# Routing the head mixture in two halves of eight token tiles, inside the neighbouring blocks

## The chip, the cores and the metric

The kernel runs on one core of one Trainium2 chip. The metric is the device time of one execution in microseconds (us). The core has five engines with queues of their own: PE (matrix products, its weight loads shown apart as PEld), DVE (vector work), ACT (activations, copies, scaling), POOL (elementwise work, here mostly powers and splits) and SP (issues DMAs). They meet only at semaphores and at barriers.

## The reference

Two layers over a batch of 4 sequences of 2048 tokens with 256 features. Layer 0 is a wave mixer with a residual and a layer norm, and then the head mixture that the change touches; layer 1 (a state-space scan and a small mixture of experts) stays as it is. What the head mixture computes for x, the output of the first layer norm:

```
logits = normalize(x) @ normalize(sim) - sigmoid(gates)      # 16 experts per token
gated  = relu(logits);  mask = gated > 0
if no expert of a token is active: mask = the 2 largest logits
rw     = softmax(where(mask, gated, -inf))                   # routing weights
q,k,v  = sum over experts of rw[e] * (x @ W_e)               # 3 x 64 columns per expert
attn   = causal softmax(q k^T / 8) v
y      = sum over experts of rw[e] * (attn @ O_e)
x      = layer_norm(x + y)
```

## The kernel before

Layer 0 runs once for each of the 4 sequences, in a loop on the device. Tokens lie in 16 tiles of 128. The names in the code: `tok` holds the tokens (16 tiles of 128x256), `xT` their transpose, `simn` the normalized expert directions, `wmoh` the expert weights as a rounded part and a remainder, `rw` the routing weights.

An iteration is a row of blocks. A block gives each engine an order of its own, and no engine goes to the next block before all have ended the present one (a barrier). The blocks that matter, in order:

- **The wave branch's second block.** PE makes the output projection tile by tile into six PSUM banks, `bank(i % 6)`; DVE adds each to `tok` and, group by group of four tiles, takes statistics (`ln1.statistics`) and scales (`ln1.scale`, L106); POOL makes the roots between them (`ln1.root`, L100); PE transposes the scaled group (L119) and ACT copies the transposes to `xT` (`ln1.copy`, L126), two tiles at a time.
- **The gating block** (L544 to L611). ACT squares and sums all 16 tiles (L558), POOL takes one root of all 16 sums (L566), PE makes the logits of all tiles (L549, against `simn` padded to 128 columns), and DVE turns them into `rw` in one chain of operations on all tiles (L574 to L611), with one exponential by ACT (L561).
- **The tile loop.** For each of 16 tiles, ACT rounds a tile of `xT` (`round_x`, L713), POOL makes its remainder (L639), PE makes six slabs of 512 columns, six matmuls each (L663), and the weighted sum over the experts is taken by ACT for experts 0 to 3 (`weigh`, L721) and by DVE for 4 to 15 (L689), followed by L695 to L702 and, two tiles later, L676 and L678. PE works one tile ahead: a slab of tile i waits until the slab of tile i-1 in its bank has been read (semaphores `pa` and `pu`). `flip` transposes q and k of the tile before into banks 6 and 7.
- The attention and output blocks, which the change leaves alone.

The order on each engine is written out by hand; no scheduler moves anything.

Of the kernel before, what the change touches and what calls it, by code (L numbers as in the profile page):

```python
# [10 lines left out]
ALU = mybir.AluOpType  # L11
# [140 lines left out]
def layer0(nc, t, out, top, tile, sem, sems, clear, bank, ident, ones, half_pow, layer_norm, kpad, x2_dram,  # L152
           x2T_dram):
    with ExitStack() as L:
# [190 lines left out]
        tok = tile(L, "tok", [P, TILES, D])  # L345
        with nc.Fori(0, BATCH) as b:
            with ExitStack() as s:
                wave_branch(nc, t, b, s, tile, sem, bank, ident, tok, xT, wqkvg, bq, bg_half, bout, wout, toep,
                            cct, layer_norm)
            with ExitStack() as s:  # L350
                head_mixture(nc, t, b, s, tile, sem, bank, ident, half_pow, tok, xT, wmoh, wo, simn, gate_sig, causal,
                             ident_bf,
                             layer_norm, x2_dram, x2T_dram)
            clear(outside)


def wave_branch(nc, t, b, s, tile, sem, bank, ident, tok, xT, wqkvg, bq, bg_half, bout, wout, toep, cct,
                layer_norm):
# [3 lines left out]
    dep_late = tile(s, "dep_late", [P, 2, CHUNK])  # L362
    tmp = tile(s, "feat_tmp", [P, 2, 5, CHUNK])
    qf = tile(s, "qf", [P, 2, CHUNK])
# [3 lines left out]
    lastg = tile(s, "lastg", [P, KC])  # L368
    proj, feat, used = sem("proj_ready"), sem("feat_ready"), sem("proj_used")
# [75 lines left out]
    wd, mm, su = sem("wave_done"), sem("wout_ready"), sem("wout_used")  # L445
    ln1 = layer_norm("ln1", s, tok, xT)
    with nc.Block() as block:
        @block.tensor
        def _(pe):

# [21 lines left out]
            for i in range(TILES):  # L472
                pe.wait_ge(wd, i // 4 + 1)
                if i >= 6:
                    pe.wait_ge(su, i - 5)
                for k in range(KC):
                    last = pe.matmul(bank(i % 6)[:, 0:D],
                                     qg[:, k, i * P:(i + 1) * P], wout[:, k, :], start=(k == 0), stop=(k == KC - 1))
# [7 lines left out]
        def _(act):  # L486
# [3 lines left out]
            for g in range(TILES // 4):  # L490
                ln1.copy(act, g)

        @block.gpsimd
        def _(pool):
            for g in range(TILES // 4):
                ln1.root(pool, g)

        @block.vector
        def _(dve):
# [16 lines left out]
            for g in range(TILES // 4):  # L516
                for i in range(4 * g, 4 * g + 4):
                    dve.wait_ge(mm, i + 1)
                    dve.tensor_tensor(tok[:, i, :], tok[:, i, :], bank(i % 6)[:, 0:D], ALU.add).then_inc(su, 1)
# [6 lines left out]
def head_mixture(nc, t, b, s, tile, sem, bank, ident, half_pow, tok, xT, wmoh, wo, simn, gate_sig, causal, ident_bf,  # L526
                 layer_norm, x2_dram, x2T_dram):
# [9 lines left out]
    with ExitStack() as g:  # L537
# [3 lines left out]
        ss, rs = tile(g, "ss", [P, TILES]), tile(g, "rs", [P, TILES])  # L541
        sq = tile(g, "sq", [P, 2, D])
        sr, sp_, lr, le, lx = (sem(n) for n in ("norm_sums", "norm_root", "logits_mm", "logits", "logits_exp"))
        with nc.Block() as block:  # L544
            @block.tensor
            def _(pe):
                for i in range(TILES):
                    for k in range(KC):
                        last = pe.matmul(bank(0, 4)[:, i * P:(i + 1) * P], xT[:, k, i * P:(i + 1) * P],  # L549
                                         simn[:, k, :], start=(k == 0), stop=(k == KC - 1))  # L550
                last.then_inc(lr, 1)

            @block.scalar
            def _(act):
                for i in range(TILES):
                    if i >= 2:
                        act.wait_ge(sr, i - 1)
                    act.activation(sq[:, i % 2, :], tok[:, i, :], ACT.Square, accum_out=ss[:, i:i + 1])\  # L558
                       .then_inc(sr, 1)
                act.wait_ge(le, 1)  # L560
                act.activation(ex[:, :, :], lg[:, :, :], ACT.Exp).then_inc(lx, 1)  # L561

            @block.gpsimd
            def _(pool):
                pool.wait_ge(sr, TILES)
                pool.tensor_tensor(rs[:, :], ss[:, :], half_pow[:, :], ALU.pow).then_inc(sp_, 1)  # L566

            @block.vector
            def _(dve):
                def wide(a):  # L570
                    return a.unsqueeze(2).broadcast_to([P, TILES, EXPERTS])

                dve.wait_ge(sp_, 1)
                dve.tensor_scalar(rs[:, :], rs[:, :], 1e-12, None, ALU.max)  # L574
                dve.drain()
                dve.reciprocal(rs[:, :], rs[:, :])
                dve.drain()
                dve.wait_ge(lr, 1)
                dve.tensor_tensor(lg[:, :, :], bank(0, 4).rearrange("p (i e) -> p i e", e=P)[:, :, 0:EXPERTS],
                                  wide(rs[:, :]), ALU.mult)  # L580
                dve.drain()
                dve.tensor_tensor(lg[:, :, :], lg[:, :, :],
                                  gate_sig[:, :].unsqueeze(1).broadcast_to([P, TILES, EXPERTS]), ALU.subtract)\
                   .then_inc(le, 1)
                dve.drain()

                for i in range(TILES):
                    dve.max(top8[:, i, :], lg[:, i, :])
                dve.drain()
                dve.tensor_copy(best[:, :], top8[:, :, 0])  # L590
                dve.drain()
                dve.memset(top8[:, :, 2:8], -3e38)
                dve.drain()
                for i in range(TILES):
# [1142 lines left out]
```

## Time and profile before

| | |
|---|---|
| median of 3 runs | 4489.09 us (4488.7 to 4492.88) |
| the profiled execution | 4494.44 us |
| its span, first to last instruction | 4492.6 us |
| mean granted TensorE clock | 0.925 of full |
| PE, DVE, POOL, ACT busy | 80%, 72%, 40%, 31% of the span |

The shares are averages over stages with very different limits: a long scan in layer 1, and the short stages of layer 0 around the change. The change must be read from its own stage, in which most engines stand still. Times below are from the span's start; the second of the four iterations stands for all, and what differs in the others is shown.

### The profile page before, as it was taken

How to read it: one execution, taken by the hardware profiler on the slowest of the kernel's cores; microseconds unless marked ns; L12 is line 12 of the kernel's file. 1: busy time of each engine (PE TensorE's matmuls, PEld its weight loads, DVE VectorE, ACT ScalarE, POOL GpSimd, SP SyncE). 2: the span in 40 equal slices, each digit the busy share in tenths (PEclk: the TensorE clock that was granted, in tenths of full speed). 3: DMA queues.
4: the chain of work that ended last, by engine and by line, in shares of the span. 5: the costliest groups of instructions: out<-in, count | busy, mean ns of one | idle time of the engine just before them, and what ended most of it. 6: DMA issues, size and time to landing. Idle time of an engine off the chain costs nothing. (4 is left out here: it accounts for less than half of the span.)

```text
span 4492.6 us, 39616 instructions
## 1 busy us (share of the span) xinstructions
PE 3576.0 (80%) x13112; PEld 2012.1 (45%) x13168; DVE 3243.8 (72%) x4803; ACT 1407.8 (31%) x2360; POOL 1796.4 (40%) x874
## 2 busy tenths in 40 slices
PE   5799879987988798777778677777777786777769
PEld 2577557765766486632223322224322233222234
DVE  4566456545754476469997679995699976799955
ACT  3222322232223222253332343331533323433310
POOL 1101210121003000309995049991099950499910
PEclk9899989998989899899999889998999998899989
DMA  3000100010001000206663136661066631366530
GB/s 126 1 19 1 57 1 10 10 57 1 1 20 58 1 1 19 90 11 217 209 206 131 34 123 211 210 202 61 10 218 209 207 131 35 122 209 209 204 107 7
DMA packets 156471, 421.74 MB, mean 94 GB/s; under 512 B 21713, under 2 KB 58961, under 8 KB 154465
## 3 DMA queue, kind: packets, MB, share of 16 engines
q1 hardware_dynamic: 156258, 419.03, 27.4%
q8 instruction: 118, 1.93, 0.2%
q14 instruction: 95, 0.78, 0.1%
HBM read 392.20 MB, written 26.78 MB: 93 GB/s over the span
## 5 line engine op out<-in xcount | busy, mean ns | idle before, releaser
L1376 POOL TENSOR_TENSOR hc<-h,c_sb 128x1024 f32<-128x1024 f32 x344 | 806.0, 2352 | 622.5 <-DMA c_sb<-bc_rows 550.7
L1304 PE MATMUL PS<-hc,ident 128*128 128x512 f32 x1376 | 712.4, 644 | 89.7 <-POOL hc L1376 75.0
L1345 ACT ACTIVATE da<-dt,a_neg 128x1024 f32<-128x1024 f32 x384 | 437.7, 1141 | 501.5 <-DVE h L1401 501.4
L1287 PE MATMUL PS<-bc,pick 128*128 128x512 bf16 x712 | 237.5, 414 | 300.6 <-DVE h L1401 265.8
L1384 DVE TENSOR_TENSOR PS<-dtu,PS 128x1024 f32<-128x1024 f32 x384 | 461.4, 1202 | 5.4 <-PE PS L1287 5.4
L1304 PEld LDWEIGHTS PS<-hc,ident 128*128 128x128 f32 x1376 | 257.7, 200 | 425.2 <-issue 207.8
L1401 DVE TENSOR_TENSOR_SCAN h<-da,state,PS 128x1024 f32<-128x1024 f32 x192 | 443.3, 2328 | 0.0
L1401 DVE TENSOR_TENSOR_SCAN h<-da,PS 128x1024 f32<-128x1024 f32 x192 | 431.3, 2268 | 0.0
L100 POOL TENSOR_TENSOR ln_rstd<-ln_var,eps_pow 128x4 f32<-128x4 f32 x65 | 71.4, 1105 | 849.8 <-DVE ln_var L93 849.8
L689 DVE SCALAR_TENSOR_TENSOR acc<-PS,rw,acc 128x192 f32<-128x192 f32 x768 | 285.0, 413 | 174.5 <-ACT acc L721 91.1
L1376 POOL TENSOR_TENSOR tok<-h,c_sb 128x1024 f32<-128x1024 f32 x168 | 395.1, 2352 | 33.7 <-DVE h L1401 24.5
L1304 PE MATMUL PS<-tok,ident 128*128 128x512 f32 x672 | 345.2, 638 | 44.7 <-POOL tok L1376 39.0
L885 POOL TENSOR_TENSOR mix<-attn,rw 128x1024 f32<-128x1024 f32 x64 | 121.3, 1904 | 517.5 <-POOLq L753 464.4
L1287 PEld LDWEIGHTS PS<-bc,pick 128*128 128x128 bf16 x768 | 57.9, 103 | 588.4 <-DVE h L1401 501.5
L663 PE MATMUL PS<-wmoh_hi,xhi 128*128 128x512 f32 x768 | 250.6, 408 | 49.1 <-POOL xlo L639 49.1
L392 PE MATMUL PS<-xT,wqkvg 128*128 128x512 f32 x512 | 234.9, 622 | 57.1 <-issue 28.2
L663 PE MATMUL PS<-wmoh_lo,xhi 128*128 128x512 f32 x768 | 243.5, 398 | 0.0
L663 PE MATMUL PS<-wmoh_hi,xlo 128*128 128x512 f32 x768 | 243.0, 398 | 0.0
L1091 PE MATMUL PS<-u,w_dt 128*128 128x512 f32 x512 | 230.9, 609 | 12.4 <-DVE dt L1217 12.4
L639 POOL TENSOR_TENSOR xlo<-xT,xhi 128x256 fp32r<-128x256 f32 x64 | 46.8, 735 | 450.3 <-ACT xhi L713 450.3
L1304 PEld LDWEIGHTS PS<-tok,ident 128*128 128x128 f32 x672 | 126.3, 200 | 203.6 <-POOL tok L1376 97.9
L1352 ACT ACTIVATE state<-h 128x1 f32<-128x1 f32 x256 | 51.9, 203 | 474.3 <-DVE h L1401 474.3
(251 smaller groups left out, 6552.1 us busy)
## 6 DMA issues: line engine op xcount, KB each, us to landing
c_sb<-bc_rows SPq DMA_DIRECT2D x512, 512.0 KB, 4.2
bu<-bc_rows SPq DMA_DIRECT2D x64, 512.0 KB, 5.4
tok<-bc_rows SPq DMA_DIRECT2D x64, 512.0 KB, 5.5
xT<-in_xT SPq DMA_DIRECT2D x5, 2048.0 KB, 7.5
tok<-in_x SPq DMA_DIRECT2D x4, 2048.0 KB, 9.6
x_after_layer<-tok SPq DMA_DIRECT2D x16, 512.0 KB, 3.0
xT_after_layer<-x2T_out SPq DMA_DIRECT2D x16, 512.0 KB, 2.8
x2T<-xT_after_layer SPq DMA_DIRECT2D x16, 512.0 KB, 3.7
```

What stands on the lines that cost most here:

```text
L100: pool.tensor_tensor(rstd[:, w], var[:, w], eps_pow[:, w], ALU.pow).then_inc(rstd_ready, 1)
L392: last = pe.matmul(bank(4 * (u % 2) + kind), wqkvg[:, k, m * P:(m + 1) * P], xT[:, k, n * CHUNK:(n + 1) * CHUNK], start=(k == 0), stop=(k ...
L663: last = pe.matmul(bank(j), x[:, i % 2, k, :], wmoh[part][:, k, j * CHUNK:(j + 1) * CHUNK], start=(q == 0), stop=(q == len(passes) - 1))
L689: op = dve.scalar_tensor_tensor(acc[:, i % 2, e % 4, :], expert(e), rw[:, i, e:e + 1], acc[:, i % 2, e % 4, :], ALU.mult, ALU.add)
L885: pool.tensor_tensor(mix[:, i % 2, :, :], attn[:, i, :].unsqueeze(1).broadcast_to([P, EXPERTS, EHD]), rw[:, i, :].unsqueeze(2).broadcast_t ...
L1091: last = pe.matmul(bank(where + j)[0:rows, :], weights(k), u[:, k, n * CHUNK:(n + 1) * CHUNK], start=(k == 0), stop=(k == KI - 1))
L1287: op = pe.matmul(bank(at + j), pick[:, row, :], bc3[:, half * HALF + j * CHUNK:half * HALF + (j + 1) * CHUNK], start=True, stop=True)
L1304: op = pe.matmul(bank(Y + j), ident[:, :], hc_at[v % 3][:, j * CHUNK:(j + 1) * CHUNK], start=(n == 0), stop=(n == N - 1))
L1345: act.activation(decay_at(v), dt[:, m, at], ACT.Exp, scale=a_neg[:, n:n + 1]).then_inc(dr, 1)
L1376: pool.tensor_tensor(hc_at[v % 3], h[:, v % 3, :], c_sb[:, v % 3, :], ALU.mult).then_inc(hr, 1)
L1384: dve.tensor_tensor(b_bank(v), dtu[:, m, at], b_bank(v), ALU.mult).then_inc(bd, 1)
L1401: dve.tensor_tensor_scan(h[:, v % 3, :], decay_at(v), bu_at[on_pool.index(v) % 2] if v in on_pool else b_bank(v), first, ALU.mult, ALU.add ...
```

## The change

It does five things. The squares and sums of the norms are taken by ACT in the wave branch's second block, four tiles behind each scaled group, and the roots by POOL in four operations of four columns, in that block too. The logits of tiles 0 to 7 are made there by PE as well, with 16 columns in place of 128, into bank 5, so the output projection has five banks. The gating block is gone. The chain that makes `rw` is called twice, each time for eight tiles: at the head of DVE's tile loop, and between its tiles 0 and 1. The logits of tiles 8 to 15 are made by PE behind the slabs of tile 0, into bank 7.

```diff
+            def logits(g):
+                pe.wait_ge(ln1.copied, 2 * g + 2)
+                for i in range(4 * g, 4 * g + 4):
+                    for k in range(KC):
+                        last = pe.matmul(bank(5)[:, i * EXPERTS:(i + 1) * EXPERTS], xT[:, k, i * P:(i + 1) * P],
+                                         simn[:, k, 0:EXPERTS], start=(k == 0), stop=(k == KC - 1))
+                last.then_inc(lr, 1)
...
-                if i >= 6:
-                    pe.wait_ge(su, i - 5)
+                if i >= 5:
+                    pe.wait_ge(su, i - 4)
...
+            logits(0)
+            logits(1)
             ln1.transpose(pe, 2)
             ln1.transpose(pe, 3)
...
             for g in range(TILES // 4):
+                act.wait_ge(ln1.done, g + 1)
+                for i in range(4 * g, 4 * g + 4):
+                    if i >= 2:
+                        act.wait_ge(sr, i - 1)
+                    act.activation(sq[:, i % 2, :], tok[:, i, :], ACT.Square, accum_out=ss[:, i:i + 1])\
+                       .then_inc(sr, 1)
                 ln1.copy(act, g)
...
+            def norm(g):
+                w = slice(4 * g, 4 * g + 4)
+                pool.wait_ge(sr, 4 * g + 4)
+                pool.tensor_tensor(rs[:, w], ss[:, w], half_pow[:, w], ALU.pow).then_inc(sp_, 1)
+
             for g in range(TILES // 4):
                 ln1.root(pool, g)
+                if g >= 2:
+                    norm(g - 2)
+            norm(TILES // 4 - 2)
+            norm(TILES // 4 - 1)
...
                     for j in range(SLABS):
+                        if i == 0 and j == 5:
+                            pe.wait_ge(lt, 1)
...
+                    if i == 0:
+                        logits(2)
+                        logits(3)
+                    if i == 2:
+                        pe.wait_ge(lt, 2)
...
+                gating(0)
                 for i in range(TILES):
+                    if i == 1:
+                        gating(1)
...
                 def weigh(i):
+                    if i % (TILES // 2) == 0:
+                        act.wait_ge(gd, 1 + i // (TILES // 2))
...
                 round_x(0)
                 round_x(1)
+                exp_logits(0)
                 for i in range(TILES):
                     weigh(i)
                     if i + 2 < TILES:
                         round_x(i + 2)
+                    if i == 0:
+                        exp_logits(1)
```

`gating(half)` holds the statements of the old DVE chain, with every slice narrowed to eight tiles; it signals `lt` once the logits have been read from PSUM and `gd` once `rw` stands. `exp_logits(half)` is the old exponential, of eight tiles.

ACT's queue from the wave branch's second block to the second tile of the tile loop, in the kernel before:

```order
L126 ACTIVATE xT<-PS 128x2x256 x8
L447 UNCONDITIONAL_BRANCH
L553 UNCONDITIONAL_BRANCH
L558 ACTIVATE sq,ss<-tok 128x256 x16
L561 ACTIVATE ex<-lg 128x256
L544 UNCONDITIONAL_BRANCH
L708 UNCONDITIONAL_BRANCH
L713 ACTIVATE xhi<-xT 128x256 x2
L721 ACTIVATE acc<-PS,rw 128x192 x4
```

The same stretch of ACT's queue in the changed kernel (L510 is the square, L126 the copy to `xT`, L735 the rounding, L756 the exponential, L745 `weigh`):

```order
L510 ACTIVATE sq,ss<-tok 128x256 x4
L126 ACTIVATE xT<-PS 128x2x256 x2
L510 ACTIVATE sq,ss<-tok 128x256 x4
L126 ACTIVATE xT<-PS 128x2x256 x2
L452 UNCONDITIONAL_BRANCH
L730 UNCONDITIONAL_BRANCH
L735 ACTIVATE xhi<-xT 128x256 x2
L756 ACTIVATE ex<-lg 128x128
L745 ACTIVATE acc<-PS,rw 128x192 x4
L735 ACTIVATE xhi<-xT 128x256
L756 ACTIVATE ex<-lg 128x128
```

The squares now stand between the copies, four ahead of each pair, and the second exponential ahead of the second tile's weighing.

DVE's queue behind tile 0 of the tile loop, in the kernel before (L699 and L702 end tile 0, L689 is tile 1's weighted sum):

```order
L699 TENSOR_TENSOR v<-acc 128x64
L702 TENSOR_TENSOR qk<-acc 128x256
L689 SCALAR_TENSOR_TENSOR acc<-PS,rw,acc 128x192 [waits weighed_by_act,slab_ready]
L689 SCALAR_TENSOR_TENSOR acc<-PS,rw,acc 128x192 [waits slab_ready]
L689 SCALAR_TENSOR_TENSOR acc<-PS,rw,acc 128x192 x2
```

The same place in the changed kernel (L721 and L724 end tile 0, L661 onward is the gating chain of tiles 8 to 15):

```order
L721 TENSOR_TENSOR v<-acc 128x64
L724 TENSOR_TENSOR qk<-acc 128x256
L661 TENSOR_SCALAR rs<-rs 128x8 [waits norm_root]
L663 RECIPROCAL rs<-rs 128x8
L666 TENSOR_TENSOR lg<-PS,rs 128x128 [waits logits_mm]
L669 TENSOR_TENSOR lg<-lg,gate_sig 128x128
L675 MAX top<-lg 128x8 x8
L677 COPY best<-top 128x8
```

Tile 1's weighted sum now stands behind the whole second gating chain, which itself waits for PE's logits.

PE's queue at the end of tile 0's slabs, in the kernel before:

```order
L663 MATMUL PS<-wmoh_hi,xhi 128x512 x2
L663 MATMUL PS<-wmoh_lo,xhi 128x512 x2
L663 MATMUL PS<-wmoh_hi,xlo 128x512 x2
L663 MATMUL PS<-wmoh_hi,xhi 128x512 [waits weighed_by_act,x_lo_ready]
L663 MATMUL PS<-wmoh_hi,xhi 128x512
```

And in the changed kernel (L631 is a matmul of the slabs, L616 one of the logits):

```order
L631 MATMUL PS<-wmoh_hi,xhi 128x512 [waits logits_taken]
L631 MATMUL PS<-wmoh_hi,xhi 128x512
L631 MATMUL PS<-wmoh_lo,xhi 128x512 x2
L631 MATMUL PS<-wmoh_hi,xlo 128x512 x2
L616 MATMUL PS<-simn,xT 128x16 x16
L631 MATMUL PS<-wmoh_hi,xhi 128x512 [waits weighed_by_act,x_lo_ready]
L631 MATMUL PS<-wmoh_hi,xhi 128x512
```

The last slab of tile 0 waits until DVE has read the first half's logits, and sixteen matmuls of 16 columns stand ahead of tile 1. (Each f32 matmul of these lists is two MATMUL records in the trace.)

## Rows read from the trace of the kernel before

**Rows 1.** Timeline of PE, first and second iteration (start us, us, engine, line, operation, [idle before])
```profile
181.75 1.22 PE L663 MATMUL PS<-wmoh_hi,xhi 128*128 128x512 f32 x2 [11.47 <-POOL xlo L639]
...
588.06 9.76 PE L477 MATMUL PS<-wout,qg 128*128 128x256 f32 x44 [1.26 <-DVE qg L514]
...
611.44 3.48 PE L119 MATMUL PS<-ident,tok 128*128 128x128 f32 x16 [3.99 <-DVE tok L106]
615.85 7.38 PE L549 MATMUL PS<-simn,xT 128*128 128x128 f32 x64 [0.94 <-PEq L447]
636.37 1.22 PE L663 MATMUL PS<-wmoh_hi,xhi 128*128 128x512 f32 x2 [13.13 <-POOL xlo L639]
```

**Rows 2.** Timeline of ACT, first and second iteration
```profile
191.98 0.42 ACT L713 ACTIVATE xhi<-xT 128x256 fp32r<-128x256 f32 x1 [4.84 <-PE PS L663]
...
606.18 1.08 ACT L126 ACTIVATE xT<-PS 128x512 f32<-128x512 f32 x2 [4.88 <-PE PS L119]
...
614.95 0.60 ACT L126 ACTIVATE xT<-PS 128x512 f32<-128x512 f32 x1 [0.26 <-PE PS L119]
615.83 0.42 ACT L558 ACTIVATE sq<-tok 128x256 f32<-128x256 f32 x1 [0.28 <-PEq L447]
...
634.70 0.72 ACT L713 ACTIVATE xhi<-xT 128x256 fp32r<-128x256 f32 x2 [7.41 <-PEq L544]
...
647.86 0.42 ACT L713 ACTIVATE xhi<-xT 128x256 fp32r<-128x256 f32 x1 [5.23 <-PE PS L663]
...
664.84 0.42 ACT L713 ACTIVATE xhi<-xT 128x256 fp32r<-128x256 f32 x1 [4.86 <-PE PS L663]
```

**Rows 3.** Timeline of POOL, second iteration
```profile
622.41 2.90 POOL L566 TENSOR_TENSOR rs<-ss,half_pow 128x16 f32<-128x16 f32 x1 [10.99 <-ACT sq L558]
...
635.59 1.41 POOL L639 TENSOR_TENSOR xlo<-xT,xhi 128x256 fp32r<-128x256 f32 x2
```

**Rows 4.** Timeline of DVE, second iteration
```profile
610.01 2.83 DVE L106 TENSOR_SCALAR tok<-tok,ln_mv,ln_rstd 128x256 f32<-128x256 f32 x8
625.34 0.17 DVE L574 TENSOR_SCALAR rs<-rs 128x16 f32<-128x16 f32 x1 [12.50 <-POOL rs L566]
...
626.93 1.32 DVE L588 MAX8 top<-lg 128x8 f32<-128x16 f32 x16
...
628.84 0.09 DVE L595 MATCH_VALUE_LOAD rep<-top,lg 128x8 f32 x1
...
631.31 0.29 DVE L597 TENSOR_SCALAR fb<-rep 128x256 f32<-128x256 f32 x1
...
633.92 0.43 DVE L611 TENSOR_TENSOR rw<-ex,ss 128x256 f32<-128x256 f32 x1
642.80 0.42 DVE L689 SCALAR_TENSOR_TENSOR acc<-PS,rw,acc 128x192 f32<-128x192 f32 x1 [8.46 <-ACT acc L721]
...
649.81 0.42 DVE L702 TENSOR_TENSOR qk<-acc 128x256 f32<-128x256 f32 x1
```

**Rows 5.** Single lines over the run (ns min/median/max, first and last start us)
```profile
L100 POOL TENSOR_TENSOR ln_rstd<-ln_var,eps_pow x65: 1006/1017/1247, 140.0 to 4487.0; 128x4 f32<-128x4 f32 x65
L676 DVE TENSOR_TENSOR q_parts<-PS,q_parts x64: 294/295/295, 211.4 to 1696.6; 64x128 fp32r<-64x128 f32 x64
```

**Rows 6.** PE timeline of the wave branch's convolution, second iteration
```profile
572.86 9.52 PE L462 MATMUL PS<-toep,dpad 128*32 128x512 f32 x128 [0.58 <-DVE dpad L505]
```

**Rows 7.** Windows, second iteration (us, busy time per engine and count, PEclk, DMA share, GB/s)
```profile
607.45:611.40 3.95, 0.00 (x0) 0.00 (x0) 3.65 (x14) 0.00 (x0) 1.22 (x1) 1.00 0.00 0
611.40:615.80 4.40, 3.48 (x16) 2.70 (x16) 1.38 (x4) 2.39 (x4) 0.02 (x1) 0.61 0.00 0
636.30:642.50 6.20, 6.13 (x14) 4.78 (x15) 0.00 (x0) 1.34 (x4) 0.70 (x2) 0.50 0.01 3
656.20:782.00 125.80, 121.41 (x537) 97.92 (x535) 89.46 (x248) 31.58 (x101) 9.57 (x13) 0.99 0.00 1
```

**Rows 8.** The page's groups: busy us, mean ns | idle of the engine before them, releaser
```profile
L663 PE MATMUL PS<-wmoh_hi,xhi 128*128 128x512 f32 x768 | 250.6, 408 | 49.1 <-POOL xlo L639 49.1
```

More of the change, by code:

```diff
@@ L368, in wave_branch @@
     lastg = tile(s, "lastg", [P, KC])
+    first = s.enter_context(ExitStack())
+    dep_late = tile(first, "dep_late", [P, 2, CHUNK])
+    tmp = tile(first, "feat_tmp", [P, 2, 5, CHUNK])
+    qf = tile(first, "qf", [P, 2, CHUNK])
     proj, feat, used = sem("proj_ready"), sem("feat_ready"), sem("proj_used")
@@ L445, in wave_branch @@
     wd, mm, su = sem("wave_done"), sem("wout_ready"), sem("wout_used")
+    sr, sp_, lr = (sem(n) for n in ("norm_sums", "norm_root", "logits_mm"))
+    first.close()
+    sq = tile(s, "sq", [P, 2, D])
     ln1 = layer_norm("ln1", s, tok, xT)
@@ L518, in _ @@
                     dve.wait_ge(mm, i + 1)
-                    dve.tensor_tensor(tok[:, i, :], tok[:, i, :], bank(i % 6)[:, 0:D], ALU.add).then_inc(su, 1)
+                    dve.tensor_tensor(tok[:, i, :], tok[:, i, :], bank(i % 5)[:, 0:D], ALU.add).then_inc(su, 1)
                 ln1.statistics(dve, g)
@@ L540, in head_mixture @@
         best = tile(g, "best", [P, TILES])
[L541 to L594, printed above, removed]
-                    dve.match_replace(rep[:, i, :], top8[:, i, :], lg[:, i, :], 1e30)
-                dve.drain()
-                dve.tensor_scalar(fb[:, :, :], rep[:, :, :], 1e29, None, ALU.is_gt)
-                dve.tensor_scalar(best[:, :], best[:, :], 0.0, None, ALU.is_le)
-                dve.drain()
-                dve.tensor_tensor(fb[:, :, :], fb[:, :, :], wide(best[:, :]), ALU.mult)
-                dve.wait_ge(lx, 1)
-                dve.scalar_tensor_tensor(ex[:, :, :], lg[:, :, :], 0.0, ex[:, :, :], ALU.is_gt, ALU.mult)
-                dve.drain()
-                dve.tensor_tensor(ex[:, :, :], ex[:, :, :], fb[:, :, :], ALU.add)
-                dve.drain()
-                dve.tensor_reduce(ss[:, :], ex[:, :, :], AX.X, ALU.add)
-                dve.drain()
-                dve.reciprocal(ss[:, :], ss[:, :])
-                dve.drain()
-                dve.tensor_tensor(rw[:, :, :], ex[:, :, :], wide(ss[:, :]), ALU.mult)
@@ L614, in head_mixture @@
-    with ExitStack() as g:
+        sp_, lr, lt, le, lx = (sem(n) for n in ("norm_root", "logits_mm", "logits_taken", "logits", "logits_exp"))
+        gd = sem("weights_done")
         acc = tile(g, "acc", [P, 2, 4, QKV])
@@ L651, in flip, with logits @@
                     last.then_inc(qt, 1)
+                def logits(g):
+                    for i in range(4 * g, 4 * g + 4):
+                        at = (i - TILES // 2) * EXPERTS
+                        for k in range(KC):
+                            last = pe.matmul(bank(7)[:, at:at + EXPERTS], xT[:, k, i * P:(i + 1) * P],
+                                             simn[:, k, 0:EXPERTS], start=(k == 0), stop=(k == KC - 1))
+                    last.then_inc(lr, 1)
                 passes = [(x, part, k) for x, part in ((xhi, 0), (xhi, 1), (xlo, 0)) for k in range(KC)]
```

59 lines of the change are left out of this document (51 added, 8 removed).

## The prediction

> **What bounds the kernel now.** I read the page first, for the span, then the timelines of the four engines between the wave branch and the tile loop of the second iteration, then windows for the granted clock. The page says only that no engine is full; what counts is which wait ends last in this stage. Around the change the kernel is a serial chain that hands the work from engine to engine. ACT ends its last copy at 614.95 + 0.60 = 615.55 and, behind the barrier, starts the squares at 615.83 [rows 2]; POOL starts the root of all sixteen at 622.41 [rows 3]; DVE starts the gating at 625.34 and ends it at 633.92 + 0.43 = 634.35 [rows 4]; ACT rounds at 634.70 [rows 2], POOL makes two remainders from 635.59 [rows 3], and PE starts the slabs at 636.37, 13.13 us after its own logits ended [rows 1]. PE is the only heavy engine of what follows and is the one kept waiting: over the four iterations it idles 49.1 us ahead of the first slab [rows 8], with its 7.38 us of logits [rows 1] beside the squares on top. From the first slab on, the tile loop is paced by PE: 121.41 busy of 125.80 us, while DVE has 89.46 [rows 7].
>
> I call T0 the start of the tile loop's block (ACT's first rounding), 634.70 now. PE starts at T0 + 1.67.
>
> **The change, part by part.**
>
> *The squares move behind the scaled groups.* Sixteen take 622.41 - 615.83 = 6.58 us, so a group of four takes 1.65 [rows 2, 3]. The first two groups cost nothing: ACT idles 4.88 us ahead of its copies there [rows 2]. The last two lie on the path. DVE scales groups 2 and 3 in one run of 2.83 us from 610.01, so group 2 is done near 611.4 and group 3 at 612.84 [rows 4]. ACT: squares 611.4 to 613.05, two copies (1.08 for two [rows 2]) to 614.15, squares to 615.8, copies to 616.9. It ends 1.35 us later than the 615.55 of now. PE's transposes are ready before ACT asks for them.
>
> *The roots.* A root of four columns takes 1.02, at most 1.25 us [rows 5]. Three of the four have cover: the one for group 0 stands ahead of the last layer-norm root, but its sums are there some 9 us earlier, and POOL is idle. The last starts at 615.85 and ends between 616.9 and 617.1, beside ACT's last copies. With the barrier (0.35 from DVE's end to ACT's start now, [rows 2, 4]) T0 becomes 617.1 + 0.3 = 617.4. **That is 634.70 - 617.4 = 17.3 us earlier.** The 2.90 us root of 16 columns, the squares, DVE's 9.01 us of gating and one barrier are all out of the path ahead of T0.
>
> *Logits of the first half, on PE.* They fill the gap in which PE now stands idle, 3.99 us ahead of 611.44 [rows 1]; only the second four wait for ACT's copies, which the squares delay from 607.26 [rows 2] to about 608.9. In the trace they are 32 records. Even at the 0.115 us each of the 128-column ones (7.38 / 64 [rows 1]) tiles 4 to 7 end by 610.8. If they end later, up to 1.7 us of it is covered by ACT's squares of group 2. Cost 0.
>
> *Five banks in place of six.* PE makes a tile of the projection in 4 x 9.76 / 44 = 0.89 us [rows 1] and now waits for the add five tiles back. Tile 5 would start at 592.5, tile 9 at 596.0; in between DVE has only one statistics group, of some 2 us, and behind tile 10 PE waits for the scaled group anyway. Cost 0; what hides it is that wait.
>
> *Gating of the first half, now inside the tile loop.* DVE's chain takes 634.35 - 625.34 = 9.01 us. Halved, the maxima save 0.66 of 1.32, the replacements half of 631.31 - 628.84 = 2.47, so 1.2 [rows 4], and seven operations of 256 elements at 0.43 [rows 4] go to the 0.295 that one of 128 elements takes [rows 5], 0.9 together. That leaves 6.2 us. Behind it on DVE's queue is tile 0's weighted sum, and ACT's four scalings wait for it too, at most 1.7 us (0.42 each, as its 256-element rounding takes [rows 2]). So DVE can start its sum at T0 + 7.9. Now it starts at 642.80, T0 + 8.1 [rows 4], since the slabs come no earlier: the gating hides behind PE's first slabs. PE's tile 0 needs only that the logits have been read before slab 5, at about T0 + 1.1. Cost 0. Uncovered it would be 6.2.
>
> *Logits of the second half.* This is the part that I put on the path: 32 records on PE between tile 0 and tile 1, where PE is the pace. The trace has no run of 16-column f32 matmuls in a stream. The nearest from above are the 128-column ones, 0.115 each, 3.7 us. Matmul time follows the columns (256 take 0.222, 128 take 0.115 [rows 1]), which would make 16 columns 0.014 each, 0.5 us, but every record has a weight load of 128x128 of its own, so something holds above that. The convolution's mixed records on 32-column weights come every 9.52 / 128 = 0.074 us [rows 6]. I take 0.074: **2.4 us per iteration**, bounds 0.5 and 3.7. The Trainium skill, TensorE: Matmul & The Clock Gate, section Back-to-back issue gap, puts streams of weight load and matmul at about 81 ns each for 128 columns; by that price, called an estimate, the part would be 2.6 us. No row here shows such a stream at 16 columns.
>
> *Gating of the second half.* It starts on DVE behind tile 0, at T0 + 15.5 (649.81 + 0.42 = 650.23 now [rows 4]), just when the logits are ready (T0 + 13.2 + 2.4), and ends at T0 + 21.8. Tile 1's sum would otherwise have started at about T0 + 19, so DVE is 2.8 us late. Does PE stop? PE runs tile 1 from T0 + 15.6 to 24, and needs DVE's reads only for slab 1 of tile 2, at about T0 + 25.5; DVE has read slab 1 of tile 1 by T0 + 22.7. It has 2.5 us of every 8.6 to catch up with ((125.80 - 89.46) over 14.6 tiles [rows 7]), and is level within tile 2. ACT's second exponential waits for DVE too, with the second tile's scalings behind it, done by T0 + 19. Cost 0, cover some 2.8 us.
>
> A sentence that the sum can do without: the Trainium skill, SBUF — State Buffer, section SBUF: two separate sides, says that a DVE operation with two SBUF inputs and a GpSimd one that reads SBUF exclude each other. Gating's subtraction now falls beside POOL's first remainder, which PE's start waits for. By that rule the sum would be up to 0.3 us per iteration smaller; no row here shows those two side by side.
>
> *The clock.* The slabs start at the low level: from 636.30 to 642.50 the granted clock is 0.50 (1.2 GHz), later 0.99 [rows 7]. From the first slab to ACT's rounding at the end of tile 0 it is 647.86 - 636.37 = 11.49 us, in the first iteration 191.98 - 181.75 = 10.23, at full speed (664.84 - 647.86) / 2 = 8.49 [rows 1, 2]. PE's idle time ahead of the slabs shrinks from 13 to about 4 us (last transpose near 615.2, slab at 619.1). An idle time of 3.95 us is in the trace, and 0.61 on average is granted right after it [rows 7]. So I let tile 0 keep its time.
>
> **The sum.** 17.3 - 2.4 = 14.9 us per iteration, 59.6 in four. The profiled execution, 4494.4 us (span 4492.6), would become 4434.8; it lies 5.3 us above the median of the runs. From that median, 4489.1 - 59.6 = **4429.5 us**.
>
> **The rivals.**
> 1. *The clock stays up* through the short idle time. Tile 0 then saves 1.7 to 3.0 us per iteration, 9 in all: 4420. For it: idle falls from 13 to 4 us and PE was busy before. Against: the row of 3.95 us.
> 2. *The second gating stops PE*: DVE's 2.8 us lateness goes through, and the logits cost 3.7. 4 x (2.8 + 1.3) = 16 us back: 4446. For it: PE runs only one tile ahead. Against: the margin of some 2.8 us worked out above.
> 3. *The loop falls into another step and gives all back.* If DVE, started late, never catches up and PE waits at every tile for a bank, each of the 15 later tiles must grow by 14.9 / 15 = 0.99 us (8.6 to 9.6) to cancel the gain; 0.15 us more per tile makes it 4498, slower. Against: DVE's 2.5 us of slack per tile, and no instruction of the later tiles has changed.
> 4. *The work only changes place*: the gating turns out to be what the first tile waits for, 6.2 us exposed. 4 x 6.2 = 25 back: 4454. Against: it ends at T0 + 6.2, while the slabs pace DVE to T0 + 13 either way.
>
> **How the numbers follow.** Main case 0.52, rival 1 0.20, rival 2 0.16, rival 4 0.05, rival 3 0.04 (half of it slower), small unknowns 0.03. The range runs from rival 1 with cheaper logits, 4414, to rival 2, 4447. The three runs span 4 us, so 0.2%, 9 us, is about what can be told from no change. Faster 0.94, same 0.03, slower 0.03.
>
> **What would show it.** Right: the squares stand between the copies and the wave block's last copy ends near 617; the gating block is gone and PE's idle time ahead of the first slab falls from 49.1 to near 16 us in all; 32 logit records take about 2.4 us behind tile 0; PE has no wait on DVE in tile 2. Wrong: a clock of 1.00 in the first slabs (faster), PE waiting on DVE's reads in tiles 1 to 3 (slower), or ACT's copies ending well behind 617.

## The result, and the profile after

| | before | after |
|---|---|---|
| median of the runs, us | 4488.9 (4484.25 to 4492.88, 4 runs) | 4443.15 (4441.28 to 4445.53, 4 runs) |
| ratio of after to before | | 0.9899, 95% interval 0.9882 to 0.9916 |
| profiled execution, its span | 4494.44, 4492.6 | 4445.53, 4443.7 |
| mean granted clock | 0.925 | 0.925 |

The change made the kernel 45.7 us faster by the medians, 48.9 by the profiled executions (the one of the kernel before lies 5.5 us above its median, the changed one 2.4). Forecast was 59.6.

PE in the second iteration, timeline (start us, us, engine, line, operation, count, [idle before]):

```profile
579.03 9.76 PE L490 MATMUL PS<-wout,qg 128*128 128x256 f32 x44 [1.26 <-DVE qg L544]
...
598.24 4.55 PE L460 MATMUL PS<-simn,xT 128*128 128x16 f32 x32
602.63 4.02 PE L119 MATMUL PS<-ident,tok 128*128 128x128 f32 x16
609.89 1.22 PE L631 MATMUL PS<-wmoh_hi,xhi 128*128 128x512 f32 x2 [3.24 <-POOL xlo L597]
...
619.96 0.62 PE L631 MATMUL PS<-wmoh_hi,xlo 128*128 128x512 f32 x2
620.42 3.64 PE L616 MATMUL PS<-simn,xT 128*128 128x16 f32 x32
623.91 0.70 PE L631 MATMUL PS<-wmoh_hi,xhi 128*128 128x512 f32 x2
624.45 0.87 PE L631 MATMUL PS<-wmoh_lo,xhi 128*128 128x512 f32 x2
625.12 1.05 PE L631 MATMUL PS<-wmoh_hi,xlo 128*128 128x512 f32 x2
```

ACT in the same stretch, its last copies, the rounding at T0 and the scalings:

```profile
606.71 1.06 ACT L126 ACTIVATE xT<-PS 128x512 f32<-128x512 f32 x2
608.21 0.72 ACT L735 ACTIVATE xhi<-xT 128x256 fp32r<-128x256 f32 x2 [0.44 <-PEq L452]
...
615.61 1.35 ACT L745 ACTIVATE acc<-PS,rw 128x192 f32<-128x192 f32 x4 [4.60 <-DVE rw L698]
620.62 0.42 ACT L735 ACTIVATE xhi<-xT 128x256 fp32r<-128x256 f32 x1 [3.65 <-PE PS L631]
```

The two stages are set against each other by the output projection, whose first matmul the change leaves alone. From it to T0 it was 634.70 - 588.06 = 46.64 us [rows 1, 2]; now it is 608.21 - 579.03 = 29.18. T0 comes 17.5 us earlier, and 17.6 to 18.0 in the other three iterations. PE's idle time ahead of the first slab fell from 13.13 to 3.24 us here, and over the run, in the page's row of the slabs, from 49.1 [rows 8] to:

```profile
L631 PE MATMUL PS<-wmoh_hi,xhi 128*128 128x512 f32 x768 | 252.3, 410 | 12.7 <-POOL xlo L597 12.7
```

Not all of it is kept. ACT rounds a tile of `xT` whenever PE has ended a tile, so its roundings measure the tiles. Tile 0 ends 620.62 - 609.89 = 10.73 us behind the first slab (11.49 before [rows 1, 2]; means over four iterations 10.54 and 10.85). Tile 1 takes 13.5 us in every iteration, 8.37 before, and later tiles 8.62, 8.59 before. The windows from the last transposes to tile 1 (us, busy time per engine and count for PE, PEld, DVE, ACT, POOL, then granted clock, DMA share, GB/s):

```profile
602.60:606.60 4.00, 3.87 (x17) 3.15 (x17) 1.20 (x4) 3.95 (x17) 1.62 (x2) 0.50 0.00 0
606.70:609.85 3.15, 0.00 (x0) 0.00 (x0) 1.43 (x3) 1.79 (x6) 2.67 (x4) 0.50 0.00 0
609.90:614.80 4.90, 4.90 (x12) 3.92 (x13) 4.25 (x33) 0.31 (x1) 0.62 (x1) 0.54 0.00 0
614.90:620.40 5.50, 5.50 (x25) 4.45 (x24) 3.61 (x12) 1.35 (x4) 0.00 (x0) 1.00 0.00 0
620.50:624.00 3.50, 3.50 (x34) 3.50 (x33) 2.49 (x9) 0.42 (x1) 0.73 (x1) 1.00 0.02 5
624.00:628.20 4.20, 4.20 (x13) 3.29 (x13) 3.50 (x32) 1.04 (x3) 0.00 (x0) 0.59 0.00 2
628.40:634.00 5.60, 5.60 (x26) 4.47 (x25) 4.34 (x13) 0.73 (x2) 0.00 (x0) 1.00 0.00 0
```

The first row is the last sixteen transposes, which stand right behind the first half's logits: the granted clock is 0.50 there already, and they take 4.02 us. It fell while those logits ran and PE was never idle: 1.00 from 598.24 to 600.00, 0.65 on average from there to 602.60. The transposes have cover, so this fall costs nothing at T0. The fifth row is the second half's logits: PE is never idle, and the granted clock is 1.00. The sixth is the beginning of tile 1: PE is still never idle, but the granted clock is 0.59, and pairs of slab matmuls take up to 1.05 us in place of 0.63. So tile 1 pays twice: 623.91 - 620.42 = 3.49 us for the logits, and 5.16 - 3.49 = 1.7 us for a slow start that no term of the forecast held.

The account of the profiled executions: T0 gives 17.56 + 17.46 + 17.81 + 17.97 = 70.8 us. The loops, from first slab to last rounding, take 127.47 in place of 122.28 us on average, 20.8 in four. The remaining 1.1 us back lie in stages that the change leaves alone: the parts of the iterations between the tile loop and the next output projection are 4.7 us longer in all, what follows the last tile loop is 2.7 shorter, and what precedes the first output projection 0.9 shorter. That is 70.8 - 20.8 - 1.1 = 48.9. Such a part takes 284.4 to 288.7 us in all these kernels and differs by up to 3.5 us between iterations of one kernel; what moves it is open. A difference of a few microseconds between two totals is therefore read from the traced stage, from the output projection to the last rounding, before it is put down to an edit: 170.70 us on average before, 158.20 in the changed kernel.

DVE around T0 and behind tile 0, and POOL at T0:

```profile
608.23 0.93 DVE L661 TENSOR_SCALAR rs<-rs 128x8 f32<-128x8 f32 x1 [4.44 <-PEq L452]
...
609.90 0.77 DVE L669 TENSOR_TENSOR lg<-lg,gate_sig 128x128 f32<-128x128 f32 x1
...
615.28 0.29 DVE L698 TENSOR_TENSOR rw<-ex,ss 128x128 f32<-128x128 f32 x1
617.15 4.54 DVE L711 SCALAR_TENSOR_TENSOR acc<-PS,rw,acc 128x192 f32<-128x192 f32 x12 [1.57 <-ACT acc L745]
...
622.91 0.16 DVE L661 TENSOR_SCALAR rs<-rs 128x8 f32<-128x8 f32 x1
...
624.10 0.29 DVE L666 TENSOR_TENSOR lg<-PS,rs 128x128 f32<-128x128 f32 x1 [0.75 <-PE PS L616]
624.48 0.29 DVE L669 TENSOR_TENSOR lg<-lg,gate_sig 128x128 f32<-128x128 f32 x1
```

```profile
608.19 0.95 POOL L592 MEMSET v<- 128x1024 f32 x1 [0.31 <-POOLq L452]
609.10 1.42 POOL L597 TENSOR_TENSOR xlo<-xT,xhi 128x256 fp32r<-128x256 f32 x2
```

The same two DVE operations take 0.93 and 0.77 us beside POOL's fill and first remainder, and 0.16 and 0.29 behind tile 0. Two things follow: the first chain lasts 7.3 us, not 6.2, and the fill of `v` stands ahead of the remainder that PE waits for.

### The profile page after: what moved, and what is told of

The parts are those of the page before. It is cut to its first block and busy times, and to the rows that moved or that the text cites. A ratio compares the mean times of both kernels' runs of the same rounds, so it can differ in the third digit from the quotient of the medians.

```text
span 4443.7 us, 39720 instructions
## 1 busy us (share of the span) xinstructions
PE 3583.3 (81%) x13112; PEld 2014.6 (45%) x13168; DVE 3257.2 (73%) x4859; ACT 1406.3 (32%) x2364; POOL 1799.9 (41%) x886
## 5 line engine op out<-in xcount | busy, mean ns | idle before, releaser
L631 PE MATMUL PS<-wmoh_hi,xhi 128*128 128x512 f32 x768 | 252.3, 410 | 12.7 <-POOL xlo L597 12.7
L631 PE MATMUL PS<-wmoh_lo,xhi 128*128 128x512 f32 x768 | 246.6, 403 | 0.0
L631 PE MATMUL PS<-wmoh_hi,xlo 128*128 128x512 f32 x768 | 245.4, 401 | 0.0
```

Of the source, the lines that this page charges most:

```text
L631: last = pe.matmul(bank(j), x[:, i % 2, k, :], wmoh[part][:, k, j * CHUNK:(j + 1) * CHUNK], start=(q == 0), stop=(q == len(passes) - 1))
```

## The experiments

Each ran beside the kernel before. Times are medians with the ratio's 95% interval; tile lengths are the spacing of ACT's roundings, as above.

**1. Is tile 1's slow start due to the narrow matmuls?** Three edits on the changed kernel.

```diff
 e1_wide_logits: second half's logits 128 columns wide, into banks 6 and 7
-  last = pe.matmul(bank(7)[:, at:at + EXPERTS], xT[...], simn[:, k, 0:EXPERTS], ...)
+  last = pe.matmul(bank(6, 2)[:, at:at + P], xT[...], simn[:, k, :], ...)
-                    if i == 2:
+                    if i == 1:
                         pe.wait_ge(lt, 2)
 e2_no_second_logits
                     if i == 0:
-                        logits(2)
-                        logits(3)
 e10_64_columns: both halves, in the same banks 5 and 7
-  bank(7)[:, at:at + EXPERTS] ... simn[:, k, 0:EXPERTS]
+  bank(7)[:, at:at + 64]      ... simn[:, k, 0:64]
```

> The changed kernel, but the logits of tiles 8 to 15 are made with all 128 columns of simn, into banks 6 and 7. Theory A (the slow start of tile 1 comes from the stretch of narrow matmuls, in which PE streams few columns): the 32 records still take about 0.115 us each, 3.7 us, the granted clock is 1.00 in tile 1, tile 1 with the logits takes about 12.1 us in place of 13.5, and the kernel takes about 4437 us. Theory B (it is a late effect of the idle time ahead of the slabs): tile 1 is slow as before, with the logits 13.7 us, and the kernel takes 4444 us.

> The changed kernel without PE's logits of tiles 8 to 15; DVE's second gating runs on the first half's logits instead, so the routing weights of tiles 8 to 15 are not those of the reference. Theory A: both the 3.5 us of the records and the slow start go, tile 1 takes 8.4 us, 5.1 less per iteration, and the kernel takes about 4423 us. Theory B: only the 3.5 us go, tile 1 takes 10.1 us, 4429 us. Theory C (the second gating on DVE is what holds tile 1): tile 1 stays above 12 us.

> The changed kernel with 64 columns per tile in place of 16 in all the logits, in the same banks. The records take 0.11 us each either way. If 64 columns are wide enough, tile 1 with its logits takes 12.0 us as with 128 columns, and the kernel 4433 us; if the clock also stays up from the first half's logits until the slabs, tile 0 falls from 10.5 towards 8.6 us, 4426 us. If 64 columns still count as narrow: tile 1 stays at 13.5 us, 4443 us.

| | us | ratio | tile 0 (mean) | tile 1 | later |
|---|---|---|---|---|---|
| after | 4443.15 | 0.9882 to 0.9916 | 10.54 | 13.53 | 8.62 |
| 128 columns | 4433.05 | 0.9863 to 0.9893 | 10.24 | 11.98 | 8.62 |
| 64 columns | 4435.28 | 0.9864 to 0.9893 | 10.24 | 11.97 | 8.62 |
| no second logits | 4422.62 | 0.9839 to 0.9869 | 10.42 | 8.41 | 8.62 |

PE and its windows in the kernel with 128 columns, where the logits end and tile 1 begins:

```profile
614.76 3.73 PE L616 MATMUL PS<-simn,xT 128*128 128x128 f32 x32
618.25 0.71 PE L631 MATMUL PS<-wmoh_hi,xhi 128*128 128x512 f32 x2
618.81 0.63 PE L631 MATMUL PS<-wmoh_lo,xhi 128*128 128x512 f32 x2
```

```profile
615.00:618.50 3.50, 3.50 (x33) 3.50 (x32) 2.80 (x9) 0.38 (x1) 0.73 (x1) 1.00 0.02 5
618.50:626.70 8.20, 8.20 (x36) 6.56 (x36) 7.09 (x44) 1.78 (x5) 0.00 (x0) 1.00 0.00 1
```

Eight times the columns take the same time from start to start (3.49 us), and the granted clock behind them is 1.00. Tile 1 is 1.55 us shorter. Shown: the slow start came from the width of the new matmuls, and the width saves nothing. With 64 columns it is the same within the runs. There the clock is up behind the first half's logits too: eight transposes take 1.09 and 1.07 us, and yet the first slabs are slow after 3.95 us of idle:

```profile
599.09 1.09 PE L119 MATMUL PS<-ident,tok 128*128 128x128 f32 x8 [0.48 <-DVE tok L106]
601.40 1.07 PE L119 MATMUL PS<-ident,tok 128*128 128x128 f32 x8 [1.22 <-ACT xT L126]
606.42 1.22 PE L631 MATMUL PS<-wmoh_hi,xhi 128*128 128x512 f32 x2 [3.95 <-POOL xlo L597]
```

Without second logits tile 1 is 5.12 us shorter than after; 4 x 5.12 = 20.5, the difference of the medians. So the logits' own 3.5 us and the slow start behind them, 1.6 to 1.7, are what the second half costs; where the forecast had 2.4 it is 5.16.

The width alone does not hold the clock up everywhere. In the kernel of experiment 3 with all 64-column logits ahead of the slabs, they run behind 2.30 us of idle: in the first iteration the granted clock is 1.00 in their first microsecond and 0.50 from 161.2 to 164.6 with PE never idle, and in the second they run at 0.50 for 6.8 us and do not raise it (0.50 over 608.0 to 609.1, their end). Shown is that 64 and 128 columns keep a clock that is up behind busy slabs, and 16 do not.

**2. What do the moved squares do alone?** The kernel before, with only the squares and roots moved:

```diff
 before's wave block: act.activation(sq..., ACT.Square) x4 ahead of ln1.copy(act, g); norm(g) on POOL
 before's gating block: squares and root removed
-                dve.wait_ge(sp_, 1)
+                dve.wait_ge(sp_, 4)
```

> The kernel before with one part of the change: squares, sums and roots in the wave branch's block, the gating block kept with its 128-column logits and its undivided chain. If each part is worth what it takes away from the old chain, the squares and the root save 6.6 + 2.9 less the 1.4 that ACT adds, 8.1 us per iteration, and the kernel takes about 4457 us. My theory: PE's logits, 7.4 us or more and hidden behind squares and root before, end last instead; DVE's product with the logits starts some 7.6 us after the block's start in place of 10.1, so 2.5 minus 1.4 us is saved, 1 us per iteration, 4485 us.

Measured 4479.19 us, ratio 0.9975 to 0.9993. PE and DVE in the gating block:

```profile
616.28 9.85 PE L567 MATMUL PS<-simn,xT 128*128 128x128 f32 x64 [1.42 <-PEq L452]
636.61 1.22 PE L671 MATMUL PS<-wmoh_hi,xhi 128*128 128x512 f32 x2 [10.49 <-POOL xlo L647]
```

```profile
626.16 0.42 DVE L587 TENSOR_TENSOR lg<-PS,rs 128x256 f32<-128x256 f32 x1 [9.38 <-PE PS L567]
```

The squares leave the block, and DVE waits nearly as long for the logits: its product with them starts 9.9 us behind PE's first logit, 10.1 before; 7.6 was expected. They take 9.85 us in place of 7.38 [rows 1], since they start at the low clock: 0.50 from 616.28 to 619, 0.59 to 622, then 1.00, where the kernel before has 1.00 from 615.85 on. From the start of the output projection, 587.21, to the first slab it is 49.40 us, where it was 636.37 - 588.06 = 48.31 [rows 1]: the stage is a microsecond longer. The run is faster all the same, 8.5 us by the medians, in part since from first slab to last rounding it takes 120.28 us, not 122.28: a later tile takes 8.427 us, not 8.589. That is 8.0 in four iterations, less 3.9 for the stage; the other 4.4 lie outside it, where the three parts between tile loop and next output projection take 853.4 us in place of 859.1. This kernel allocates some buffers elsewhere too, which experiment 5 shows to move the pace of a tile, so its shorter tiles need not be a gain of the squares. So T0's 17.5 us are no sum of gains that each move has by itself: the squares alone bring nothing as long as the logits and the gating stand in their old block.

**3. Can the logits stand at a better place?** The 16-column ones ahead of the slabs; one behind every second slab matmul of tile 0; of the 64-column ones a half, or all, ahead of the slabs (with the fill of `v` behind the remainders).

```diff
 e4_logits_ahead; e12_all_ahead the same with 64 columns; e11_half_ahead moves logits(2) alone
+                logits(2)
+                logits(3)
                 for i in range(TILES):
...
                     if i == 0:
-                        logits(2)
-                        logits(3)
 e5_spread_logits
+                            if i == 0 and q % 2 == 1 and 3 * j + q // 2 < 16:
+                                logit(3 * j + q // 2)
```

> The changed kernel with the logits of tiles 8 to 15 ahead of tile 0's slabs in PE's queue, where PE waits 1.68 us for the first remainder anyway. The 3.5 us of records then hide 1.7 of themselves: slabs start about 3.6 us after the block's start, tile 1 takes 8.4 us. Theory A: a stretch of narrow matmuls leaves the clock low, tile 0 stays at 10.5 us, net 3.2 us less per iteration, 4430 us. If work of any kind keeps the clock up, tile 0 falls towards 8.6 us, and the kernel to about 4423 us.

> The changed kernel with the sixteen 16-column logit matmuls of tiles 8 to 15 not in one stretch behind tile 0 but one behind every second matmul of tile 0's slabs. Theory A (a stretch of narrow matmuls lowers the clock): no such stretch is left, tile 1 takes 8.4 us at a granted clock of 1.00; tiles 0 and 1 together take 10.3 + 3.5 + 8.4 = 22.2 us in place of 24.0, or less if the weight loads hide beside the wide matmuls; about 4436 us. If it is the weight loads themselves and not their being together that lower the clock, the two tiles stay at 24 us and the kernel at 4443 us.

> A version put together from what the runs showed: 64 columns in all logits (e10), the memset of v behind the first two remainders (e7), and the logits of tiles 8 to 11 ahead of tile 0's slabs, those of tiles 12 to 15 behind them. At the high level the 16 records ahead take 1.75 us and end 0.4 us after the first remainder is there; 1.8 us leave tile 1. If the dense records right after the barrier also keep the clock up, tile 0 falls from 10.3 to 8.6 us: 4428 - 4 x (1.4 + 1.7) = 4416 us. If the clock has already fallen by then, they take 3.5 us, the slabs start 2.1 us later and nothing is won: 4429 us.

> As e11_half_ahead, but all logits of tiles 8 to 15 stand ahead of tile 0's slabs. Clock up: 3.6 us ahead, slabs 2.2 us later, 3.6 us off tile 1, tile 0 at 8.6 us: 4428 - 4 x (1.4 + 1.7) = 4416 us. Clock low: 7 us ahead as in e4_logits_ahead, of which 64 columns might raise the clock by the time the slabs start: slabs 5.6 us later, 3.6 us off tile 1, 1.8 off tile 0, about 4429 us.

| | us | ratio | tile 0 | tile 1 |
|---|---|---|---|---|
| 16 columns ahead | 4437.73 | 0.9873 to 0.9904 | 11.1 to 11.3 | 8.40 |
| 16 columns spread | 4454.37 | 0.9901 to 0.993 | 15.7 to 22.6 | 8.39 to 9.25 |
| half of 64 ahead | 4430.86 | 0.9854 to 0.9887 | 9.6 to 11.1 | 10.19 |
| all of 64 ahead | 4438.93 | 0.9877 to 0.991 | 9.7 to 10.1 | 8.40 |

PE with the 16-column logits ahead, and its windows of them and of the first slabs:

```profile
606.14 6.98 PE L616 MATMUL PS<-simn,xT 128*128 128x16 f32 x32 [1.42 <-PEq L452]
612.96 1.20 PE L633 MATMUL PS<-wmoh_hi,xhi 128*128 128x512 f32 x2
```

```profile
606.10:613.00 6.90, 6.86 (x33) 6.89 (x33) 5.88 (x37) 1.03 (x3) 2.32 (x3) 0.50 0.00 0
613.10:618.00 4.90, 4.90 (x13) 3.84 (x13) 0.30 (x2) 0.73 (x2) 0.00 (x0) 0.50 0.02 3
```

The idle time ahead of the slabs is filled, yet the logits cost nearly double at the low clock, 0.213 us each (6.82 us from their start to the first slab), and behind 6.9 busy us the slabs still start at 0.50. Spread out, they keep tile 0 slow: the windows of its slabs in that kernel are

```profile
618.00:623.00 5.00, 5.00 (x17) 4.23 (x17) 2.55 (x17) 0.76 (x3) 0.00 (x0) 0.50 0.00 0
623.00:628.00 5.00, 5.00 (x23) 4.32 (x24) 1.49 (x4) 0.70 (x2) 0.00 (x0) 0.75 0.01 3
```

That was a miss: by the median it is the slowest variant of the changed kernel, and its six runs spread from 4438.27 to 4457.77 us. A closed stretch of narrow matmuls is not needed; one among every two slab matmuls kept the clock low as well.

Whether the place ahead of the slabs is better is not shown. With 16 columns the medians differ by 5.4 us, but the intervals overlap and the traced stage is 158.87 us on average, against 158.20 in the changed kernel: the slabs start 5.1 us later, as much as tile 1 gains, and tile 0 takes 0.7 us more. The lower total comes from the parts outside the stage (854.8 against 863.8 us for the three between iterations). With 64 columns all ahead costs 3.7 us over the 64-column kernel by the medians, again with overlapping intervals, and 0.5 us per iteration in the stage (156.82 against 156.29). The half ahead is no better than the kernel of experiment 4, which leaves all behind the slabs (4430.86 against 4428.55; stage 156.12 against 156.06). The 4416 us that two expectations named needed a clock that stays up, and it did not.

**4. The fill of `v`, and the division of the gating.** In the 128-column kernel the fill goes behind the first two remainders; in the kernel without second logits, one chain of 16 tiles takes the place of the two.

```diff
 e7_wide_memset_last
-                pool.memset(v[:, :, EHD:P], 0.0)
                 for i in range(TILES):
+                    if i == 2:
+                        pool.memset(v[:, :, EHD:P], 0.0)
 e9_undivided_gating
-                gating(0)
+                gating()
...
-                    if i == 1:
-                        gating(1)
```

> The kernel of e1_wide_logits with POOL's memset of v behind its first two remainders instead of ahead of them. If POOL and DVE keep each other out of SBUF, DVE's first operation falls from 0.93 us to 0.17, since no memset runs beside it. The first remainder then waits only for ACT: slabs start 1.2 us after the block's start in place of 1.67, which is worth 0.5 us per iteration, 2 us in all: 4431 us against 4433, too small for the totals and to be read from the trace.

> The kernel of e2_no_second_logits (no logits of tiles 8 to 15; the first half's stand in for them, so those routing weights are not the reference's) with one gating chain of 16 tiles at the head of DVE's tile loop in place of two of 8. If the first tile's slabs hide 9 us of gating as well as 6, the kernel takes what e2 took, 4422 us, tile 1 takes 8.4 us and tile 2 falls from 8.7 to 8.6 us. If dividing it is what makes the hiding possible, PE stops for DVE in tile 1, some 3 us per iteration: 4434 us.

With the fill moved, POOL and DVE at T0:

```profile
604.09 1.47 POOL L598 TENSOR_TENSOR xlo<-xT,xhi 128x256 fp32r<-128x256 f32 x2 [0.82 <-ACT xhi L739]
605.50 0.94 POOL L594 MEMSET v<- 128x1024 f32 x1
```

```profile
603.62 0.17 DVE L662 TENSOR_SCALAR rs<-rs 128x8 f32<-128x8 f32 x1 [4.28 <-PEq L452]
...
605.84 0.64 DVE L681 COPY best<-top 128x8 f32<-128x8 f32 x1
```

The first DVE operation is short again, 0.17 us, and a copy that now falls beside the fill takes 0.64 (0.17 in the changed kernel). Both long operations end with the fill: 609.16 and 609.14 in the changed kernel, 606.48 and 606.44 here. So it was the fill. The first slab stands 1.28 us behind T0, not 1.68: 1.6 in four iterations, too little for the runs to show (4428.55 against 4433.05, 0.9853 to 0.9881 against 0.9863 to 0.9893). The undivided gating gives 4418.9 (0.9835 to 0.9861), against 4422.62 with two chains: where PE makes no second logits, as in both of these kernels, hiding the gating needs no division.

**5. Does less idle time keep the clock up?** On the 64-column kernel, the first two tiles are rounded and their remainders made in the wave branch's block; for that `xhi` and `xlo` are allocated once for the layer, and `simn` is 64 columns wide. A last run has this allocation alone.

```diff
 e13_round_early (and, the first three lines alone, e14_placement_alone)
-        simn = tile(L, "simn", [P, KC, P])
+        simn = tile(L, "simn", [P, KC, 64])
+        xhi, xlo = (tile(L, n, [P, 2, KC, P], F32R) for n in ("xhi", "xlo"))
...
                 ln1.copy(act, g)
+                if g == 0:
+                    for i in range(2):
+                        act.activation(xhi[:, i, :, :], xT[:, :, i * P:(i + 1) * P], ACT.Copy)
```

> The kernel of e10_64_columns with the rounding and the remainders of tiles 0 and 1 moved into the wave branch's block, behind the first two copies, where ACT idles 3.3 us. PE then needs nothing at the block's start: slabs start about 0.1 us after it in place of 1.67, 1.5 us per iteration, 4429 us. The idle time ahead of the slabs falls from 4.0 to about 2.4 us. If that keeps the clock up (the rival of the prediction), tile 0 also falls from 10.2 to 8.6 us: 4422 us. If the gating then shows (it ends 6 us after the start, ACT's scalings 7.5, while PE comes back for the first bank at 8.6 us at the high level), PE waits less than 1 us in tile 1.

> The run with 64 columns in all logits, and from the run with the early rounding only its allocation: the tile loop's xhi and xlo buffers are taken once at the level of the layer, and simn is 64 columns wide. Rounding and remainders stay where they are in the tile loop, so no instruction moves. If the faster slab pace of the early-rounding run (8.433 us for a later tile, against about 8.62) comes from where the operands lie, the later tiles show about 8.43 us here too and the kernel takes about 10 us less than the run with 64 columns, near 4425; tile 0 stays near 10.2 us and the first slab stands 1.7 us behind the start of the loop's block. If the pace comes from the rounding's new place instead, the later tiles stay at 8.6 us and the kernel at 4435.

| | us | ratio | tile 0 by iteration | tile 1 | later |
|---|---|---|---|---|---|
| round early | 4412.25 | 0.9822 to 0.9849 | 8.47, 8.47, 8.45, 10.95 | 11.75 | 8.433 |
| placement alone | 4425.51 | 0.9842 to 0.9875 | 10.31, 10.10, 10.03, 10.07 | 11.75 | 8.433 |
| 64 columns | 4435.28 | 0.9864 to 0.9893 | 10.28, 10.43, 10.13, 10.10 | 11.97 | 8.616 |

PE's first slab in the second and the fourth iteration with early rounding, and the windows behind each:

```profile
598.15 0.70 PE L642 MATMUL PS<-wmoh_hi,xhi 128*128 128x512 f32 x2 [2.30 <-PEq L453]
...
1471.73 1.19 PE L642 MATMUL PS<-wmoh_hi,xhi 128*128 128x512 f32 x2 [2.30 <-PEq L453]
```

```profile
598.15:602.00 3.85, 3.85 (x17) 3.20 (x18) 3.25 (x22) 0.31 (x1) 0.92 (x1) 1.00 0.00 0
...
1471.70:1476.00 4.30, 4.27 (x10) 3.43 (x11) 3.67 (x28) 0.31 (x1) 0.94 (x1) 0.50 0.00 0
```

After 2.30 us of idle the slabs start at full clock in three iterations of four and at half in one, though the rows of PE's work ahead of them read alike. In the fourth the clock fell within the idle time: 0.67 on average from 1469.4 to 1471.7, 1.00 from 595.85 to 598.10 in the second. What tells the fourth apart stays open. With the logits ahead (experiment 3, 64 columns) PE's work starts behind the same 2.30 us, and there the clock was still 1.00 in two iterations of four. The placement alone takes 9.8 us off the 64-column kernel, and its shorter tiles account for it: from first slab to last rounding 125.6 us become 123.1, 2.5 in each iteration, 10 in four. The matmuls themselves are shorter: of the slabs' row in 100 us of steady loop,

```profile
L631 PE MATMUL PS<-wmoh_lo,xhi 128*128 128x512 f32 x140 | 44.0, 395 | 0.0
```

with 64 columns, and with the allocation

```profile
L631 PE MATMUL PS<-wmoh_lo,xhi 128*128 128x512 f32 x143 | 44.4, 391 | 0.0
```

at a granted clock of 1.00 in both. Shown: where buffers lie in SBUF sets some 2% of the pace of the slabs. Which buffer, and why, was not tried. The early rounding itself is worth the other 13.3 us; 10.7 of them are in the traced stage (first slabs 1.7 us earlier behind the output projection, and the faster tile 0). The version with both is the fastest of all, 31 us below the change.

## Why the prediction was nearly right, and where it was off

- **T0.** Forecast 17.3 us earlier, measured 17.5 to 18.0. The last copy ends at 607.77, which on before's time (9.03 us later, by the output projection) is 616.8; forecast 616.9. The squares behind the first two groups, three of four roots, the first half's logits and the five banks cost nothing at T0, as argued. (The first half's logits took 4.4 us from start to start, not the 3.7 allowed for at most, and the clock fell while they ran, which the forecast didn't see; both had cover.)
- **Logits of the second half: the term that was mis-sized.** It said 0.074 us a record, 2.4 us in all. Measured 3.49, 0.109 a record. The convolution's records stand on 32-column weights; with weights of 128x128 a record of 16 columns costs what one of 128 costs. The bound of 3.7 held. The Trainium skill, TensorE: Matmul & The Clock Gate, section Back-to-back issue gap, has 81 ns for a stream with 128 columns; the runs here show 109 ns in f32 with 16, 64 and 128 columns alike, and the measurement decides.
- **The clock behind them.** No step asked what they do to the clock: 1.7 us per iteration. The prediction watched idle time alone. Both misses together are 5.16 - 2.4 = 2.76 us per iteration, 11.0 in four. The profiled gain is 10.7 under the forecast: 11.0, less T0's surplus of 1.6, plus the rest of 1.1 and 0.2 for tile 0 and the later tiles together.
- **Luck in the total.** It lies in the range, 4414 to 4447, near its upper end. That end came from rival 2, a stop of PE by DVE that didn't occur; a slow clock that no term named took about its place. The main case, 4429.5, was 13.7 us too low.
- **Gating of the first half.** 7.3 us, not 6.2, because of POOL's fill and remainder. DVE's sum starts at T0 + 8.9, not 7.9; the slabs were not held, so its price was nothing, as forecast.
- **Gating of the second half.** It waits 0.75 us for the longer logits. PE shows no wait on DVE in tiles 1 and 2; forecast held, and without the logits' time as cover tile 2 takes 8.61 to 8.89 us, up to 0.3 more, so the margin is small.
- **The shared ports.** The sentence on the Trainium skill, SBUF — State Buffer, section SBUF: two separate sides, would have let PE start later by up to 0.3 us. The subtraction did fall beside the first remainder, and DVE was the one held (0.77 us); PE started at T0 + 1.68, as before. The other row is not this case of the rule, since the held operation at T0 has one input and POOL's fill reads nothing. The same section names a second case, a DVE operation in a 2-port perf mode beside any GpSimd operation; that could fit, but no run here shows the mode.
- **Rival 1** (clock stays up) didn't occur: 3.24 us of idle, then 0.54. In the changed kernel the clock was low ahead of the idle time already, but with 64 columns it was not, and after 3.95 us the slabs were slow just the same. The early rounding shows what it is worth: tile 0 at 8.46 in three iterations, 1.7 us less than the mean with the placement alone (10.13). **Rival 2** was right that the logits cost near 3.7 and the total close to its 4446, but wrong on the cause: the stop is the clock, not DVE. **Rivals 3 and 4** didn't occur: later tiles 8.62, and no exposed gating.

## What to carry to other kernels

Small work put between two stretches of a busy TensorE can cost its instructions and not its columns (here 16, 64 and 128 columns took the same time), and can cost the clock of what follows: look at the granted clock behind it, and try it wider. When a chain of several engines is shortened, ask what waits next in each block; a single move may give nothing until the others are made. Compare an unrelated pace (here, later tiles) in every variant: a new allocation moved it by 2%, 10 us in all, as much as some edits under study. And check a difference of totals in the stage that was edited: with the 16-column logits ahead, the total fell by 5.4 us and the stage grew.

## What the runs showed of the hardware

- An f32 record with weights of 128x128 took 0.109 us with 16 columns, 0.109 with 64 and with 128 (3.49 us for 32 in each), and 0.213 with 16 or 64 at the low clock (6.82 us for 32).
- Behind 3.5 us of back-to-back 16-column matmuls that began at clock 1.00, it was 0.59 over the next 4.2 us, with PE never idle; behind 64 or 128 columns at the same place 1.00.
- At 0.50, 6.8 us of back-to-back matmuls of 16 or of 64 columns did not raise the clock; the 128-column logits of experiment 2 began at 0.50 and ended at 1.00.
- After 2.30 us of idle the clock was still 1.00 in three of four iterations of one kernel and in two of four of another; after 3.95 us of idle, from full clock too, the slabs started at 0.50 (3.1 us window; 4.9 us window of the changed kernel 0.54, after 3.24 us and from 0.50).
- A DVE operation on 8 columns took 0.93 us beside a fill by POOL and ended with it, 0.17 without.
- Allocation alone changed a tile from 8.616 to 8.433 us.
